# Splitting the first 448 score columns of each group into hi and lo parts, with part of the lo work on VectorE

## The reference, cut to what matters

```python
x = x + xattn(layernorm(x), ctx, Wq, bq, Wk, bk, Wv, bv)
# in xattn, with query = layernorm(x), ref = ctx:
Q = query @ Wq + bq
K = ref @ Wk + bk
V = ref @ Wv + bv
scores = jnp.einsum('bqh,bkh->bqk', Q, K)
attn = jax.nn.softmax(scores, axis=-1) / 16
return jnp.einsum('bqk,bkh->bqh', attn, V)
```

## Time and profile before

| | us |
|---|---|
| median of 3 runs | 237.56 |
| lowest, highest | 235.97, 237.79 |
| profiled execution, its own time | 236.64 |
| its span in the profile | 234.5 |
| TensorE busy | 222.7 (95%) |
| VectorE busy | 142.1 (61%) |
| ScalarE busy | 140.4 (60%) |
| GpSimd busy | 120.0 (51%) |

### The profile page before, as it was taken

The page is one execution under the profiler, slowest core; times in us unless marked ns, Lnnn a source line. Parts: engine busy times, 40 slices in busy tenths (PEclk is TensorE's granted clock), DMA queues, the critical chain, the costliest instruction groups (busy, mean ns, idle before and its releaser), DMA issues.

```text
span 234.5 us, 4294 instructions
## 1 busy us (share of the span) xinstructions
PE 222.7 (95%) x1603; PEld 197.5 (84%) x1603; DVE 142.1 (61%) x329; ACT 140.4 (60%) x263; POOL 120.0 (51%) x78
## 2 busy tenths in 40 slices
PE   8989999999999979789998999989999999999994
PEld 7746888888888878679988999874689999999993
DVE  2239955555555554725996776526244749987784
ACT  5147686666666666326794566736315848767570
POOL 1065788888888998230699930000000535555450
PEclk9999999999999999999999999999999999999999
DMA  6999999999999500799994000000000595970000
GB/s 196 369 429 415 413 419 415 418 418 418 413 418 421 235 0 0 283 420 426 418 422 191 3 1 0 3 0 0 3 0 0 183 349 200 412 291 6 0 0 25
DMA packets 8533, 52.95 MB, mean 226 GB/s; under 512 B 953, under 2 KB 1218, under 8 KB 6466
## 3 DMA queue, kind: packets, MB, share of 16 engines
q1 hardware_dynamic: 8514, 52.69, 56.2%
HBM read 52.56 MB, written 0.13 MB: 225 GB/s over the span
## 4 chain that ended last, share of the span: by engine, by line
PE 76%; DVE 9%; DMA 6%; ACT 4%; issue 2%; SPq 1%; POOL 1%; ACTq 0%; DVEq 0%; POOLq 0%
PE psum L455 30%; PE psum L532 14%; PE psum L765 8%; PE psum L450 7%; DMA late_sb<-in_ctx_T 6%; PE psum L509 3%; PE psum L660 3%; PE psum L647 2%; PE psum L446 2%; PE psum L689 2%; PE psum L716 1%; DVE work L1200 1%; DVE ring L1238 1%; DVE ring L1223 1%; DVE w_lo L1374 1%
## 5 line engine op out<-in xcount | busy, mean ns | idle before, releaser
L374 POOL TENSOR_TENSOR ctx_lo<-ring,ctx_hi 128x1792 fp32r<-128x1792 f32 x13 | 52.6, 4044 | 24.8 <-ACT ctx_hi L829 24.8
L438 POOL TENSOR_TENSOR h_lo<-ring,h_hi 128x512 fp32r<-128x512 f32 x16 | 24.8, 1552 | 66.9 <-ACT h_hi L1031 60.9
L455 PE MATMUL psum<-late_sb,work 128*128 128x448 f32 (+1 forms) x112 | 35.4, 459 | 1.1 <-DMA late_sb<-in_ctx_T 1.1
L455 PEld LDWEIGHTS psum<-late_sb,work 128*128 128x128 f32 x112 | 19.6, 190 | 13.9 <-issue 13.8
L836 ACT ACTIVATE probsT_hi<-psum 128x512 fp32r<-128x512 f32 (+1 forms) x28 | 13.7, 541 | 22.3 <-PE psum L450 22.3
L1091 DVE TENSOR_REDUCE smalls<-psum 128x1 f32<-128x896 f32 x14 | 15.3, 1090 | 18.4 <-PE psum L509 13.4
L455 PE MATMUL psum<-xT,late_sb 128*128 128x128 f32 x224 | 26.2, 276 | 0.1
L455 PEld LDWEIGHTS psum<-xT,late_sb 128*128 128x128 f32 x224 | 25.5, 192 | 0.3 <-DVE xT L1344 0.3
L829 ACT ACTIVATE ctx_hi<-ring 128x1792 fp32r<-128x1792 f32 x13 | 22.1, 1699 | 2.5 <-DMA ring<-in_ctx 2.5
L1115 DVE TENSOR_TENSOR probsT_lo<-psum,probsT_hi 128x512 fp32r<-128x512 f32 (+1 forms) x28 | 16.2, 619 | 6.9 <-ACT probsT_hi L836 6.9
L532 PE MATMUL psum<-ctx_hi,probsT_hi 128*128 128x256 f32 x98 | 16.7, 286 | 2.5 <-DVE probsT_lo L1115 2.5
(11 more groups left out here) (253 smaller groups left out, 472.4 us busy)
## 6 DMA issues: line engine op xcount, KB each, us to landing
late_sb<-in_ctx_T SPq DMA_DIRECT2D x14, 896.0 KB, 13.6
ring<-in_ctx SPq DMA_DIRECT2D x14, 896.0 KB, 12.2
late_sb<-in_late SPq DMA_DIRECT2D x10, 825.0 KB, 10.6
late_sb<-in_experts SPq DMA_DIRECT2D x8, 1024.0 KB, 9.8
late_slots<-in_experts SPq DMA_DIRECT2D x8, 1024.0 KB, 13.5
early_sb<-in_early SPq DMA_DIRECT2D x1, 512.0 KB, 4.2
early_sb<-in_early SPq DMA_DIRECT2D x1, 465.0 KB, 17.2
work<-in_levels SPq DMA_DIRECT2D x1, 416.0 KB, 18.4
```

The source lines that it names most:

```text
L374: nc.gpsimd.tensor_tensor(ctxNv[1][:, r % 2], ring[:, r], ctxNv[0][:, r % 2], ALU.subtract).then_inc(s["ctx_lo"], 1)
L438: nc.gpsimd.tensor_tensor(hT[1][:, e % 2, at, :], h32[:, at, :], hT[0][:, e % 2, at, :], ALU.subtract).then_inc(s["h_lo_done"], 1)
L455: last = nc.tensor.matmul(o, lhs(c), rhs(c), start=(c == 0), stop=(c == n - 1))
```

## The change

SPLIT goes from 256 to 448 columns, the whole first half of a group: its plain matmuls go and the six split ones get 448 columns. ScalarE makes the hi part of 2 x 448 columns in L849. Of the lo part GpSimd makes the first 2 x 256 columns, as before (POOL_SPLIT), and VectorE the other 2 x 192, one and a half tiles, in a new function `ctxT_lo_rest`, at the head of its iteration, ahead of `maxima`; TensorE waits for it by a new semaphore, `T_lo_rest`. For group 13 it stands between L1142 and `maxima`. VectorE's loop is written out. The semaphore `gs_done` is dropped and its signal is the third one of `x_ident`, whose first two come from GpSimd's copies ahead of it.

```diff
-SPLIT = 2 * P
+SPLIT = HALF
+POOL_SPLIT = 2 * P
...
-                nc.gpsimd.tensor_tensor(Tv[1][:, r % 2], ringT[:, r, :, 0:SPLIT], Tv[0][:, r % 2], ALU.subtract).then_inc(s["T_lo"], 1)
+                nc.gpsimd.tensor_tensor(Tv[1][:, r % 2, :, 0:POOL_SPLIT], ringT[:, r, :, 0:POOL_SPLIT], Tv[0][:, r % 2, :, 0:POOL_SPLIT], ALU.subtract).then_inc(s["T_lo"], 1)
...
-                                    s_("g").rearrange("p (h t) -> p h t", t=1).to_broadcast([P, HV, T]), ALU.mult).then_inc(s["gs_done"], 1)
+                                    s_("g").rearrange("p (h t) -> p h t", t=1).to_broadcast([P, HV, T]), ALU.mult).then_inc(s["x_ident"], 1)
...
-                last = wide(bank[b][:, plain:HALF], lambda c: G[:, c * P:(c + 1) * P], lambda c: ringT[:, r, c, plain:HALF])
+                if plain < HALF:
+                    last = wide(bank[b][:, plain:HALF], lambda c: G[:, c * P:(c + 1) * P], lambda c: ringT[:, r, c, plain:HALF])
...
                         if i == 2 * DC:
                             pe.wait_ge(s["T_lo"], g - 2)
+                            pe.wait_ge(s["T_lo_rest"], g - 2)
...
-            pe.wait_ge(s["gs_done"], 1)
+            pe.wait_ge(s["x_ident"], 3)
...
+            def ctxT_lo_rest(g, r):
+
+                dve.wait_ge(s["T_hi"], g - 2)
+                at = slice(POOL_SPLIT, SPLIT)
+                V.tensor_tensor(Tv[1][:, r % 2, :, at], ringT[:, r, :, at], Tv[0][:, r % 2, :, at], ALU.subtract).then_inc(s["T_lo_rest"], 1)
+
...
-            with dve.Fori(0, 2) as i:
-                for j in range(RING):
-                    maxima(i * RING + (j + 2), (j + 2) % RING)
-                    sums(i * RING + (j + 1), (j + 1) % 2)
-                    accumulate(i * RING + j, j % 2)
-                    probs_lo_parts(i * RING + (j + 1))
-            for g in range(2 * RING, NG - 3):
+            for g in range(NG - 3):
+                if g > 0:
+                    ctxT_lo_rest(g + 2, (g + 2) % RING)
                 maxima(g + 2, (g + 2) % RING)
...
             V.tensor_copy(ctxNv[0][:, g % 2, at], ring[:, g % RING, at]).then_inc(s["dve_chain"], 1)
             chain[0] += 1
+            ctxT_lo_rest(g, g % RING)
             maxima(g, g % RING)
```

More of the change, by code:

```diff
@@ L208, in perceiver @@
             var_done ln_sd ln_xn ln_T ln_xT q_ready q_done q_done_dve g_ready g_done qb_ready qb_done bv_ready
-            T_hi T_lo ctx_hi ctx_lo last_lo probsT_hi scores_ready max_ready exp_done alpha_done probs_transposed probsT_lo pv_done acc_done
+            T_hi T_lo T_lo_rest ctx_hi ctx_lo last_lo probsT_hi scores_ready max_ready exp_done alpha_done probs_transposed probsT_lo pv_done acc_done
             o_T o_copied att_ready
-            sd1_done xz_done xz_T xz_copied ba_done ba_read u_ready ln1p_first ln1p_exp rates_done gs_done
+            sd1_done xz_done xz_T xz_copied ba_done ba_read u_ready ln1p_first ln1p_exp rates_done
             proj_bank tap0_done conv_done silu_done z_done zs_done
```

## The result

The changed kernel takes 246.2 us (median of 4, 245.2 to 247.4), the kernel before 237.67 beside it: a ratio of 1.038, interval 1.031 to 1.045. I had forecast 242.8 us and at most 244.4. Slower was right, and so were both stalls; the size was not. Both stalls are where they were expected, and something came behind each that the forecast did not have.

What follows compares the result with a forecast made beforehand. The prediction took TensorE alone to bound the kernel from group 3's scores to about 86 us. From 236.64 us, +4.55 (group 3), -1.35 (groups 4 to 12), +2.6 (group 13) and +0.35 gave 242.8 us, range 239.6 to 244.4.

Steps and rivals of the forecast that it cites:

- both stalls: TensorE waits for VectorE's new low part at its first use, group 3 (+4.55 us), and its last, group 13 (+2.6 us).
- The lock-out in group 3: At the first use GpSimd's running L374 blocks VectorE's new instruction till 31.29 us, so attend begins 4.55 us later.
- The turn in group 13: In the last group GpSimd's L392 goes before VectorE's new part, +2.6 us; VectorE first, +0.35, was a rival at 27%.
- It starts 0.14 us later, does two low terms in 0.40 and begins attend: Group 3: TensorE restarts 0.14 us after the new part, takes 0.40 for two low-part matmuls, begins attend at 32.24 us.
- Groups 4 to 12: Steady groups, where VectorE's new part falls into GpSimd's gap: nine groups gain 0.15 us each, -1.35 us (1.1 to 1.5).
- the upper bound of the forecast: Time of one widened split matmul on TensorE, in proportion to its columns: 0.207 us, where the forecast took 0.199.
- the middle: Steady groups: 0.15 us gained a group, between 0.17 if nothing is late and 0.12 if the new part is late.
- The edits at cost 0: ScalarE's high part, 0.32 us longer but covered by a wait, VectorE's written-out loop and the merged semaphore cost nothing.
- some tenths at worst: VectorE's written-out loop fetches more instructions, at worst some tenths, and beside its idle time.
- The sum: Whole kernel: 236.64 + 4.55 - 1.35 + 2.6 = 242.4 us for the profiled execution, plus 0.35 for all executions: 242.8 us.

Runs made afterwards that it cites:

- Experiment 6: The changed kernel, with GpSimd's instructions on the plain context made to wait for VectorE's new part, so VectorE always goes first: 237.55 us, ratio 1.006.
- experiment 1: The changed kernel, with matmuls of no use put into TensorE's two stalls, in groups 3 and 13: 242.95 us, ratio 1.026.
- experiment 4: The changed kernel, with VectorE's part of group 13 moved to where GpSimd has its gap, taking the last stall away: 242.36 us, ratio 1.022.
- experiment 5: The changed kernel, with GpSimd alone making group 3's low part and VectorE's part of group 13 moved to GpSimd's gap: 236.27 us, ratio 0.999.
- experiment 3: The changed kernel, with GpSimd making group 3's whole low part and VectorE beginning with group 4: 239.76 us, ratio 1.014.

## Why the prediction was wrong

**The lock-out in group 3: right.** The forecast was that the new part is issued 0.6 us after the start of GpSimd's L374 and ends 0.41 us after its end. It was issued 0.93 us after that start and ended 0.41 us after that end. Experiment 6 shows that it is the turn that costs, as the same instruction at the same place takes 0.55 us.

**The turn in group 13: right.** The page "SBUF — State Buffer" of the Trainium skill (Who interferes with whom: the one that issues first holds the pair for its whole instruction) gave the right side here, where VectorE's two instructions followed each other with no gap and GpSimd, issued during the first, went before the second.

**"It starts 0.14 us later, does two low terms in 0.40 and begins attend": this step failed, and with it the sum.** It took TensorE to go on after a stall at the rate that it had before. It starts 0.14 us later, but the two low terms take 0.88 us from their start to that of the next step, and the attend and transposes behind them 5.65 instead of 3.27 us, because the granted clock had fallen to 1.2 GHz. The same went behind the last stall. The missing term is 2.38 + 0.96 us behind the stalls and some 0.4 us within them; taking it away with matmuls of no use gave back 3.6 us between spans, 2.8 by the ratios (experiment 1). The rows of before could not show it, as their clock was full in every slice with gaps of 1.24 us in TensorE's work; the page's row of the granted clock was full, and I read that as a constant. The Trainium skill (TensorE: Matmul & The Clock Gate, Why this matters for your kernels) warns of idle gaps between bursts of matmuls, and I had a gap of 4 us in hand and did not look. This trace agrees for the gap of 4.06 us; the 2.55 us gap and, in one execution, one of 1.24 us were followed by the lower clock as well.

**Groups 4 to 12: right in sign, half in size.** 1.35 us were forecast; the rows give 0.62 over eight periods, 0.08 a group. Two terms have a part in it: a split matmul over 448 columns starts 0.208 us after the one ahead (1.24 / 6 in the chain), not 0.199. That is the upper bound of the forecast, the rate of the 256-column ones in proportion. And the new part is late in every second group, which costs 0.06 us there. The forecast had this at 0.05 and took the middle, so most of the miss is the rate of the matmuls, 6 x 0.009 = 0.05 us a group.

**The edits at cost 0: right.** The written-out loop measured 1.000, though the "some tenths at worst" of the forecast came from no row; ScalarE's L852 took 0.95 to 0.96 us and TensorE never waited for it.

**The sum.** The forecast for the profiled execution was 242.4 us, and it took 246.09, 3.7 more: 3.34 for the slow clock behind the stalls, 0.33 for stalls of 7.48 instead of 7.15 (7.06 in experiment 1, where the clock stayed full), 0.71 that the groups from 4 on did not give, 0.06 behind attend(13), less 0.74 for the start. So the slow clock is the error in the main, and without the early start it would have been larger. The medians are only 8.5 us apart, the spans 9.5: three of the four executions of the kernel before in this first set lie at 237.56 to 237.79, where in the later sets 10 of 63 lie above 237.5. That the number came as near as it did is in part luck.

## What to carry to other kernels

Price a new stall of TensorE twice: once for its length, once for the time that the work behind it takes at the lower clock, here 2.4 us behind 4.06 and 1.0 behind 2.55; matmuls of no use in the gap took the second price away, and so did making the stall short (the full clock in eight of ten executions of experiment 6). An instruction of VectorE with two inputs in SBUF beside a busy GpSimd must be looked at in each place where it runs, the first and last of a loop above all, because the steady groups had a gap for it and these two had not. Where the order can't be seen to, give the short instruction the turn with a semaphore, as experiment 6 does.

## What the runs showed of the hardware that I had not expected

The lower clock did not need the long stall: behind a wait of 1.24 us the profiled execution of experiment 4 ran at 0.50 from 106 to 109 us, while the profiled executions of the kernel before and of experiment 5 had the same wait and a full clock. Nor did it always fall in the gap: worked out from the granted clock of short stretches, it fell 0.6 us before TensorE started again in group 3 of the changed kernel, 0.15 us after it in group 13, 0.5 us after it in the last attend of experiment 4, and 1.4 us after it in group 13 of experiment 3.

Why the clock fell behind that short wait in one execution and not in others stays open.

The split matmuls take 0.118 us for 256 columns and 0.208 for 448, 0.46 ns a column at either width; a record of a plain one takes 0.84. A plain product is two records and so 1.68 ns a column, three split ones are 1.39. So the 192 columns that the change moved are worth by this 0.64 - 0.53 = 0.11 us a group on TensorE, for 0.55 us more work on VectorE and 0.32 on ScalarE.
